# Early weight rounding, a lag of five and four shifted buffers in the first stage of a four-layer kernel

## What is computed

```python
# layer 0: cond mixes channels with a matrix per batch entry, ffn is a rank-16 adapter of the best of 8 experts
out = einsum('boi,bih->boh', agg_w, x) + agg_b
logits = einsum('bsd,ed->bse', out, route_w);  best, idx = top_k(logits, 1)
h = einsum('bsd,erd->bser', out, A)
x = x + einsum('bser,eor->bso', onehot(idx) * best * h, Bw)
# layer 1: cond is a grouped convolution of 9 taps along the row, ffn an int8-like product
out = conv(x, weight, groups=4) + ctx + bias
CB, SCB = quantize_rowwise(W)            # round(w * 127 / max|w| of the row)
x = x + (round(out * 127 / rowmax) @ CB.T) * rowmax / 127 * SCB / 127 + bias
# layers 2 and 3: convolution and top-2 adapters; mixing, an MLP of 2048 and a latent branch fc1, expert_w, fc2
```

## Time and profile before

| what | value |
|---|---|
| median of three executions | 1695.0 us |
| profiled execution / span | 1696.1 / 1694.4 us |
| PE busy | 1592.4 us (94%) |
| DVE, ACT, POOL busy | 832.7, 506.6, 314.2 us |
| first stage | 0 to 212.1 us |
| second block begins | 213.2 us |
| mean granted clock of PE | 0.976 |

### The profile page before, as it was taken

The page is one execution under the profiler, slowest core; times in us unless marked ns, Lnnn a source line. Parts: engine busy times, 40 slices in busy tenths (PEclk is TensorE's granted clock), DMA queues, the critical chain, the costliest instruction groups (busy, mean ns, idle before and its releaser), DMA issues.

```text
span 1694.4 us, 20601 instructions
## 1 busy us (share of the span) xinstructions
PE 1592.4 (94%) x7752; PEld 1294.7 (76%) x7752; DVE 832.7 (49%) x1316; ACT 506.6 (30%) x761; POOL 314.2 (19%) x262
## 2 busy tenths in 40 slices
PE   7699677999999879999999999999999999999996
PEld 5578535888987547886888888888878888888875
DVE  1676448998556455774333333332633333333336
ACT  4244223343327441222322222222232222222112
POOL 1000011134317451022121111111112111111111
PEclk9899988999999999999999999999999999999999
DMA  8383462555675675896171111111923511111115
GB/s 300 126 241 132 137 115 93 173 180 190 206 265 166 221 270 196 305 333 241 62 149 50 50 50 50 50 50 50 372 96 93 111 50 50 50 50 50 50 38 174
DMA packets 117272, 238.56 MB, mean 141 GB/s; under 512 B 22503, under 2 KB 61535, under 8 KB 115810
## 3 DMA queue, kind: packets, MB, share of 16 engines
q1 hardware_dynamic: 82042, 155.27, 27.4%
q0 software_dynamic: 23040, 68.24, 13.9%
q10 hardware_dynamic: 12112, 14.00, 2.9%
HBM read 164.51 MB, written 89.19 MB: 150 GB/s over the span
## 4 chain that ended last, share of the span: by engine, by line
PE 78%; DVE 4%; DMA 2%; issue 2%; ACT 1%; SPq 0%; ACTq 0%; POOL 0%; DVEq 0%
PE pu L1919 26%; PE pd L1919 25%; PE l_po L1919 10%; PE pf L1919 6%; PE pw L628 2%; PE pw L627 2%; PE l_ea L1281 1%; PE l_ea L1852 1%; DMA scratch_g<-latent_out 1%; PE l_po L1852 1%; PE pg L1057 1%; PE l_tr L1867 1%; DVE row_peak L900 1%; DMA delta<-scratch_expert_out 1%; PE l_ea L1867 1%
## 5 line engine op out<-in xcount | busy, mean ns | idle before, releaser
L1919 PE MATMUL pd<-down_hi,hid_hi 128*128 128x512 f32 x640 | 249.1, 389 | 2.9 <-issue 2.9
L1919 PE MATMUL pu<-y_hi,up_hi 128*128 128x512 f32 x640 | 250.6, 392 | 0.6 <-issue 0.6
L1919 PE MATMUL pu<-y_lo,up_hi 128*128 128x512 f32 x640 | 250.3, 391 | 0.0
L1919 PE MATMUL pu<-y_hi,up_lo 128*128 128x512 f32 x640 | 250.2, 391 | 0.0
L1919 PE MATMUL pd<-down_hi,hid_lo 128*128 128x512 f32 x640 | 249.0, 389 | 0.0
L1919 PE MATMUL pd<-down_lo,hid_hi 128*128 128x512 f32 x640 | 249.0, 389 | 0.0
L2220 DVE TENSOR_TENSOR hid_lo<-hidden,hid_hi 128x512 fp32r<-128x512 f32 x64 | 44.3, 693 | 391.5 <-ACT hid_hi L2128 391.5
L2050 POOL TENSOR_TENSOR down_lo<-raw,down_hi 128x1024 fp32r<-128x1024 f32 x40 | 100.4, 2510 | 681.5 <-ACT down_hi L2065 681.5
L2122 ACT ACTIVATE hidden<-pu 128x512 f32<-128x512 f32 x64 | 38.3, 598 | 471.7 <-PE pu L1919 471.7
L2159 DVE TENSOR_TENSOR acc<-pd,acc 128x512 f32<-128x512 f32 x224 | 143.6, 685 | 54.7 <-PE pd L1919 51.4
L1919 PEld LDWEIGHTS pd<-down_hi,hid_hi 128*128 128x128 f32 x640 | 120.1, 188 | 28.5 <-issue 3.7
(11 more groups left out here) (317 smaller groups left out, 2520.5 us busy)
## 6 DMA issues: line engine op xcount, KB each, us to landing
X<-scratch_x SPq DMA_DIRECT2D x256, 64.0 KB, 2.5
l_x<-scratch_x SPq DMA_DIRECT2D x32, 512.0 KB, 6.4
delta<-scratch_expert_out SPq DMA_DIRECT2D x32, 512.0 KB, 6.8
raw<-in_up SPq DMA_DIRECT2D x32, 512.0 KB, 3.8
raw<-in_down SPq DMA_DIRECT2D x32, 512.0 KB, 4.4
y1T<-in_x SPq DMA_DIRECT2D x16, 512.0 KB, 8.6
scratch_x<-y1T SPq DMA_DIRECT2D x16, 512.0 KB, 3.0
scratch_x<-l_x SPq DMA_DIRECT2D x16, 512.0 KB, 5.5
```

Source lines behind the costliest of these rows:

```text
L1919: mm = pe.matmul(out, lhs[a], rhs[b], start=first and n == 0, stop=last and n == len(pairs) - 1)
```

## The change

- W is loaded ahead of x tiles 4 to 7. DVE makes all eight row peaks, the scales and all eight roundings before the loop. PE and ACT transpose and copy W in steps 0 to 3. The scales are turned in step 3, into the convolution's banks `pv`, and copied out in step 4.
- LAG0 is 5 and X, Xs have four buffers (XS = 4). The fourth pair takes the place of the second `xT`, so heads 8 to 15 share one `xT`.
- Transposes of tiles 8 to 15 are in steps 4 to 11, their head products in steps 5 to 12. x tiles 8 to 15 are loaded behind stores 0 to 3 instead of 3 to 6.
- `exp` is loaded after head 10 instead of head 15 and has another address; `fcC` and `fcB` still wait for head 15.
- In the second block all 32 latent units run before step 0, in another order of results; ACT copies six results out before step 0 and the last two at its start. The first two x1 loads wait for four results, and DVE's first addition for all eight.
- The blank rows are stored three at a time: 2048 pieces of 780 bytes.

```diff
-LAG0 = 4
-TURN_AT = {s: LEAD + s - 6 for s in range(6, 6 + NT - LEAD)}
+LAG0 = 5
+XS = 4
+TURN_AT = {s: LEAD + s - 4 for s in range(4, 4 + NT - LEAD)}
-SPLIT_AT = {s: (2 * s - 4, 2 * s - 3) for s in range(2, 6)}
+SPLIT_AT = {s: (2 * s, 2 * s + 1) for s in range(4)}
...
+    names["X"], names["Xs"] = [at(n, address, [P, 2 * GROUPS, P]) for n, address in (("X3", 194496), ("Xs3", 198592))]
...
-            for t in range(1, LEAD):
+            for t in range(1, 4):
                 x_in(t)
             for c in range(4):
                 sp.dma_start(raw[:, 2 * c:2 * c + 2, :], ...)
+            for t in range(4, LEAD):
+                x_in(t)
...
-                if t - 3 in range(4):
-                    for c in (2 * (t - 3), 2 * (t - 3) + 1):
-                        sp.wait_ge(turned, 2 * (c + 1))
-                        x_in(LEAD + c)
+                for c in SPLIT_AT.get(t, ()):
+                    sp.wait_ge(turned, 2 * (c + 1))
+                    x_in(LEAD + c)
                 sp.wait_ge(x1_stored[t % 4], 16 * (t // 4 + 1))
-                if t >= 3:
-                    sp.wait_ge(conv_done, 2 * (t - 2))
-                load_windows(sp, SC["x1"], t, X[t % 3], X_loaded[t % 3])
+                if t >= XS:
+                    sp.wait_ge(conv_done, 2 * (t - XS + 1))
+                elif t == XS - 1:
+                    sp.wait_ge(h_mm, LEAD)
+                    sp.wait_ge(edges, 2 * XS)
+                load_windows(sp, SC["x1"], t, X[t % XS], X_loaded[t % XS])
...
+            pool.wait_ge(h_mm, LEAD + 3)
+            pool.dma_start(K["exp"][:], ...).then_inc(K["fc_loaded"], 16)
             pool.wait_ge(h_mm, NT)
-            pool.dma_start(K["exp"][:], ...).then_inc(K["fc_loaded"], 16)
             pool.dma_start(K["fcC"][:], fc1T[:, :, 6 * P:8 * P]).then_inc(K["fc_loaded"], 16)
...
-                if s == 6:
+                if s == LAG0 - 2:
                     turn_scales()
...
-                t = s - 3
+                t = s - LAG0 + 1
...
-            for c in range(4):
+            edge(Xs[XS - 1])
+            for c in range(KC):
                 weight_top(c)
+            weight_scales()
+            for c in range(KC):
+                weight_round(c)
             dve.wait_ge(suma_mm, 1)
...
-                if s == 0:
-                    for c in range(4, KC):
-                        weight_top(c)
-                    weight_scales()
-                for c in SPLIT_AT.get(s + 1, ()):
-                    weight_round(c)
...
-    LATENT = [6, 7, 0, 1, 2, 3, 4, 5]
+    LATENT = [0, 1, 2, 3, 6, 7, 4, 5]
...
         sp.dma_start(bias[:], A["L1_ffn_bias"].partition_broadcast(P)).then_inc(bias_loaded, 16)
+        sp.wait_ge(g_mm, 4)
...
         latent_out(0)
+        latent_out(1)
         magnitudes(0, 1)
-        latent_out(1)
         latent_out(2)
         latent_out(3)
+        latent_out(4)
         high(0)
+        latent_out(5)
         for s in range(NT):
             if s == 0:
-                latent_out(4)
-            if s == 1:
                 latent_out(6)
                 latent_out(7)
...
-        latent(0, 9)
+        latent(0, 13)
         turn(0)
-        latent(9, 14)
+        latent(13, 18)
         broadcast(0)
-        latent(14, 22)
+        latent(18, 32)
...
-                       blank[:].unsqueeze(1).to_broadcast([P, NEXP + 1, RW])).then_inc(blank_stored, 16)
+                       blank[:].rearrange("p r c -> p (r c)").unsqueeze(1).to_broadcast([P, (NEXP + 1) // 3, 3 * RW])).then_inc(blank_stored, 16)
```

More of the change, by code:

```diff
@@ L335, in head @@
                 for k in range(KC):
-                    last = pe.matmul(ph[:, 0:P + E0], xT[t % 2][:, k, :], wa[:, k, :], start=k == 0, stop=k == KC - 1)
+                    last = pe.matmul(ph[:, 0:P + E0], xT[turning(t)][:, k, :], wa[:, k, :], start=k == 0, stop=k == KC - 1)
                 last.then_inc(h_mm, 1)
@@ L448, in turned_x @@
                     if t >= 2 and i == 0:
-                        act.wait_ge(h_mm, t - 1)
-                    act.copy(xT[t % 2][:, 4 * i:4 * i + 4, :], pt[i][:].rearrange("k (p o) -> k p o", p=4)).then_inc(xT_made, 1)
+                        act.wait_ge(h_mm, t if t > LEAD else t - 1)
+                    act.copy(xT[turning(t)][:, 4 * i:4 * i + 4, :], pt[i][:].rearrange("k (p o) -> k p o", p=4)).then_inc(xT_made, 1)
             def head_out(t):
@@ L537, in conv_out, with edge @@
                                   row.unsqueeze(1).to_broadcast([P, KC, CH]), ALU.add).then_inc(y_made, 1)
-            for xs in Xs:
+            def edge(xs):
                 dve.memset(xs[0:CH, :, P - 1:P], 0.0).then_inc(edges, 1)
                 dve.memset(xs[CH:P, :, 0:1], 0.0).then_inc(edges, 1)
+            for xs in Xs[:XS - 1]:
+                edge(xs)
             dve.wait_ge(rows_loaded, 16)
@@ L683, in latent_buffers @@
     s_.sb("latent_before", [P, KC * D + 3 * D])
-    names["fcA"] = s_.sb("latent_fcA", [P, NLAT, 4 * P])
-    s_.sb("latent_between", [P, 11 * D])
+    names["exp"], names["fcA"] = s_.sb("latent_exp", [P, NLAT, NLAT * P]), s_.sb("latent_fcA", [P, NLAT, 4 * P])
+    s_.sb("latent_between", [P, 9 * D])
     names["fcB"], names["fcC"] = s_.sb("latent_fcB", [P, NLAT, 2 * P]), s_.sb("latent_fcC", [P, NLAT, 2 * P])
-    s_.sb("latent_second", [P, D])
-    names["exp"] = s_.sb("latent_exp", [P, NLAT, NLAT * P])
-    s_.sb("latent_behind", [P, 5 * D + NT * KC + 104])
+    s_.sb("latent_behind", [P, 8 * D + NT * KC + 104])
     names["g_out"] = s_.sb("latent_out", [P, 2, NLAT * P])
@@ L946, in add @@
                 if t == 0:
[L947 removed]
+                    dve.wait_ge(g_mm, KC)
                 if t >= 2:
@@ L1073, in tensor @@
                     g = group_of[s] + 1
-            if s == 2:
-                latent(26, 32)
             if s < NT:
@@ L1078, in tensor @@
                 product(s, 0)
-            if s == 0:
-                latent(22, 26)
             if s >= LAG:
@@ L1120, in l2_buffers @@
     names["war"] = at("l2_war", TABLES, [P, KC, R2 + E2])
-    names["blank"] = at("pair_blank", TABLES + 2560, [P, RW])
+    names["blank"] = at("pair_blank", TABLES + 2560, [P, 3, RW])
     names["lg"] = at("router_lg", TABLES + 2560, [P, NT, E2])
@@ L1262, in make_tables @@
     def make_tables(pool):
-        pool.memset(blank[:, 0:R2], 0.0).then_inc(tables_step, 1)
-        pool.memset(blank[:, R2:RW], float(PAIRS)).then_inc(tables_step, 1)
+        pool.memset(blank[:, :, 0:R2], 0.0).then_inc(tables_step, 1)
+        pool.memset(blank[:, :, R2:RW], float(PAIRS)).then_inc(tables_step, 1)
         pool.memset(every[:], 1.0).then_inc(tables_step, 1)
@@ L1270, in make_tables @@
         pool.wait_ge(tables_step, 4)
-        pool.dma_start(SC["pairs"].rearrange("(n p) c -> p n c", p=P),
-                       blank[:].unsqueeze(1).to_broadcast([P, NEXP + 1, RW])).then_inc(blank_stored, 16)
+        pool.dma_start(SC["pairs"].rearrange("(p n r) c -> p n (r c)", p=P, r=3),
+                       blank[:].rearrange("p r c -> p (r c)").unsqueeze(1).to_broadcast([P, (NEXP + 1) // 3, 3 * RW])).then_inc(blank_stored, 16)
     def router(pe, t):
```

34 lines of the change are left out of this document (16 added, 18 removed).

## The result

The changed kernel takes **1682.59 us** (median of 5 runs, 1678.14 to 1685.38) against 1692.64 us (1691.76 to 1698.77, 5 runs) of the kernel before on the same chip. The ratio is 0.9928, with an interval of 0.9902 to 0.9953: 0.7% faster, 10 to 12 us. The forecast was 1674 in a range of 1664 to 1686. The profiled execution took 1679.22 us, with a span of 1677.5 against 1694.4 before: 16.9 us, more than the medians show, so the table gives the difference between two single executions.

| us | before | after | gained |
|---|---|---|---|
| first mixing | 51.16 | 50.44 | 0.7 |
| first convolution | 79.00 | 73.80 | 5.2 |
| first stage ends | 212.07 | 197.07 | 15.0 |
| tile 2's high part (second block) | 278.61 | 261.79 | 16.8 |
| first convolution of the second block | 299.41 | 283.43 | 16.0 |

The account below looks back on a forecast made before the run. PE, busy 94% of the span, was taken as the bound, with only its gaps and slow-clock work to win. First stage 18.2 plus second block 2.4 gave 20.6 us, span 1673.8, execution 1675.5, median 1674; range 1664 to 1686.

Parts of the forecast that it names:

- Rounding ahead of the loop: First stage, before mixing: 24.1 us of DVE work hidden by heads 3 to 7, ending at 48.8; first mixing stays at 51.2.
- Steps 0 to 4: Early first stage: steps with two blocks of W take 5.8 us; first convolution at 78.0, before at 79.0.
- The high clock: PE in the early steps: assumed at its high clock, cost taken as 0, with 6 us as the other end.
- Steps 5 to 12: Full steps of the first stage: eight steps of 8.44 us, from 78.0 to 145.5, none waiting for windows.
- The circle of 8.44 us: Full step: convolution, head, head's copy, ACT's second shifted copy, next convolution; 8.44 us, untouched by lag and buffers.
- signs that the prediction itself had named as wrong: First mixing after 52, granted clock 0.5 between 52 and 75, ACT waiting for windows before step 12, DVE waiting for result 2.
- Tail: First stage's end: last window loads at 177.9, end 16.0 us behind, 193.9 instead of 212.1; the stage gains 18.2 us.
- SP keeps up: Rival, first stage: landing stays near 3 us, PE and additions set the end at about 184; 1664; chance 0.15.
- SP becomes the bound of all 16 tiles: Rival, first stage: ends at 61.5 + 16 c + 11.5, c the cycle; c = 9.5 gives 1705; chance 0.04 near old time, 0.03 beyond.
- Blank rows: Second block: 2048 pieces for 6144 land in 8.3 us instead of 24.9; sign of being right: under 12 us.
- Latent products: Second block: 0.3 us from magnitudes at 34.1, 2.1 us from six units no longer ahead of tile 2; gains 2.4 us.
- The later x1 loads: Second block: x1 loads land at about 24 and are needed at 45, so they cost nothing.

## Why the prediction was right, and where not

*Sign and size.* Faster was right, and the time, 1682.59, is in the range. The best value was 9 us too low: 20.6 us were forecast, the profile shows 16.9, the medians 10 to 12. So the span's gain of 16.9 is part luck of the two executions profiled. One execution stood for the kernel: five other traces with this first stage, or one with three buffers of windows or a later load (stage end 200.58 to 202.32, against 197.07) put its gain at 10 to 15 us.

*Rounding ahead of the loop: right.* W was there in time, DVE ended at 48.3 (forecast 48.8), the first mixing came at 50.44 (51.2). POOL's loads, which I had weighed against it, did not cost the path anything: the two loads beside the roundings land in 4.1 to 5.9 us where they took 4.4 to 5.0, all before the roundings end, and two roundings take 1.00 and 1.05 us instead of 0.75 and 0.69. It was DVE that waited, 0.6 us; one of the two loads landed at most 0.9 us later. What I had worked out by the rule of the Trainium skill, SBUF — State Buffer, a landing only after the last rounding, is not what this trace shows.

*Steps 0 to 4: too dear by 4.2 us.* Mixing came at 50.44, 54.17, 59.18, 64.19, 70.08: 5.0 us for a step with two blocks, where the sum had 5.7 to 5.8. The first convolution is at 73.80, not 78.0. The failing term is what was added to the span of 5.66 - 1.15 = 4.5 us: a turn, a copy and two latencies, 1.2 us in sum, of which 0.5 was real. The high clock, taken as given with 6 us of doubt, was granted (1.00 from 60 to 80). The first convolution came 5.2 us earlier than before, where the sum had 1.0.

*Steps 5 to 12: the failed step.* "The circle of 8.44 us is untouched" was true of six of the eight distances (the others 9.37 and 8.63), but "no full step waited for windows" no longer held: ACT waited 0.97 us at 89.40 and 0.22 at 106.45, one of the signs that the prediction itself had named as wrong. The store of tile 3 landed in 7.9 us, beside the first latent load at 79.99, that of tile 5 in 7.5. The sum let tile 11's window loads follow its addition by one landing of 5.0 us, 146.3 to 151.3. The addition was there at 142.31, 4.0 us earlier; the landing took 3.0; but the store had stood in SP's queue for 9.9 us, and the loads began at 155.17. The queue's backlog, left over from the early steps (an addition every 5 us, a cycle of 8.02) and from three landings of over 7 us (tiles 3, 5 and 10), was put at nothing. The early steps' error of 4.2 us the one way and this one of 8 the other partly cancel.

*Tail: nearly right.* The last window loads came at 182.65 (177.9 forecast): 4.7 us late, after 4.2 us of head start from the early steps. The end is 14.4 us behind them, not 16.0. The rival "SP keeps up" is excluded; "SP becomes the bound of all 16 tiles", given 0.07 with both its outcomes, is what happened in kind, at c = 8.0 instead of the 9.2 from which it would have been slower. Its formula, taken from the first store at 59.38, gives 59.4 + 128.3 + 11.5 = 199.2 for a measured 197.07.

*Blank rows.* Landing 13.3 instead of 8.3 us, over the 12 named as a sign; at a third of the pieces and the same bytes the time halved. It sufficed for result 2 not to hold up PE.

*Latent products: right number, by luck.* 2.4 us were forecast for the block, tile 2 shows 1.8, the next convolution 1.0. Each of its steps came out (product 0 at 33.2 for 32.7, magnitudes at 34.9 for 34.1; the rounding beside POOL is the difference of 1.6 us in the high part of tile 0, 28.5 for 26.9). What failed is that both edits were costed as one, so that two large effects hid each other. The block's own 10 us were in the blank rows, and the moved products, with POOL's additions that moved with them, gave 8 of them back. The trace of before held the clue: the six units at 272.35 cost tile 2 at most 5.16 us, 0.86 each, while ten more units ahead of product 0 at the same 0.86 are 8.6 us as soon as nothing else holds product 0 up.

*"The later x1 loads: nothing"* failed: the wait for unit 16 moved them from the block's start to 216.13, so POOL's additions fell on DVE's roundings. The bytes were hidden; the engine that used them was not.

## What to carry to other kernels

When a change holds several edits for one stretch, cost each alone against the kernel before, not only their sum: here the smallest edit gained 10 us and its neighbour took 8 of them away, and their sum looked like a plain 2. A store, its landing and the loads that read it back, on one queue, are a cycle: work out its length for every tile, beside the transfers of other queues, and try the next store ahead of the wait, with an eye on how much later the consumer then gets its loads: the same order gave 1% in one kernel and cost 2.5% in the other. Where a transfer moves, follow the engine that uses it to the work it will then run beside.

## What the runs showed of the hardware

**DVE beside POOL's arithmetic.** Eight tensor-scalar roundings in place, of 128x256 each, take 2.67 us alone and 6.18 to 6.41 us beside two additions of POOL (4.7 us) with both inputs in SBUF; the same on the next group, 128x384 each: 3.67 us alone, 5.58 to 5.75 beside one addition of 2.4 us, in all traces. The Trainium skill, SBUF — State Buffer, "Who interferes with whom", says that a tensor_scalar can enter a mode in which DVE also takes the port pair that it shares with GpSimd, and that whichever of the two begins first then keeps the other out for its whole instruction. The traces agree in kind: DVE loses 3.5 to 3.7 us of 4.7, and 1.9 to 2.1 of 2.4.

**A store beside a large load.** A store of 512 KB lands in 2.6 to 3.5 us as a rule. When POOL has put 1 or 2 MB of loads into its queue in the 6 us before it, SP's loads behind it begin only 5.8 to 9.6 us after its issue: this is so for all 25 such stores in the ten traces with SP's old order. Without such a load ahead the longest was 5.6 us, with two x tiles loading beside it.

**Small pieces.** 1.56 MB of blank rows in 6144 pieces land after 22.9 to 25.6 us (four traces), in 2048 pieces after 13.3 to 17.5 us. The copy of result 2, which waits for a latent store of another queue, comes at 24.4 to 27.2 us into the block with single rows and at 14.8 to 19.0 with threes.
